# Score tiles of an attention kernel: how five PSUM banks are shared between two passes

## What is computed

```
L1 attention  : softmax(q k^T / sqrt(128)) v, no mask, 16 key heads
L2 attention  : rotary, causal, 16 key heads
L2 ffn, part 1: rotary, causal, 4 key heads (grouped query), then experts
L3 attention  : causal, ALiBi slopes, 4 key heads
L3 ffn        : layer_norm -> w1 (ternary) -> gelu -> layer_norm -> w2 (ternary)
ternary_quant : scale = 1 / clip(mean(|w|), 1e-5); clip(round(w*scale), -1, 1) / scale
```

## Time and profile before

| | |
|---|---|
| median of three runs | 1224.3 us |
| runs | 1224.0 to 1225.42 us |
| span of the profiled execution, first to last instruction | 1215.0 us |
| median of the runs less that span | 9.3 us |
| busy: PE, DVE, ACT, POOL | 1047.8, 841.1, 673.7, 404.6 us |
| mean granted PE clock, share of full | 0.961 |

### The profile page before, as it was taken

One profiled execution on the slowest core, in us unless ns is written; L12 is line 12 of the kernel. 1 busy time (PEld: TensorE's weight loads), 2 busy tenths in 40 slices (PEclk: granted clock), 3 DMA queues, 4 the chain that ended last, 5 costly groups with the idle time before them and its releaser, 6 DMA issues.

```text
span 1215.0 us, 24466 instructions
## 1 busy us (share of the span) xinstructions
PE 1047.8 (86%) x7565; PEld 549.4 (45%) x7640; DVE 841.1 (69%) x2519; ACT 673.7 (55%) x1313; POOL 404.6 (33%) x675
## 2 busy tenths in 40 slices
PE   3468998988889987889999999998989688999886
PEld 1312232322256664445555545554556344555455
DVE  5987878687645557778788787775333766868666
ACT  2217767765754442656666666666556345666553
POOL 5622242222424533442322322334245434222112
PEclk7669999999999999999999999999999889999999
DMA  7235444341112342423412512210233321221001
GB/s 193 68 92 195 131 152 148 125 160 32 33 57 77 92 152 56 130 72 114 131 50 87 184 34 88 77 51 29 79 93 121 93 77 42 88 76 40 2 1 35
DMA packets 100054, 108.03 MB, mean 89 GB/s; under 512 B 10722, under 2 KB 86850, under 8 KB 99688
## 3 DMA queue, kind: packets, MB, share of 16 engines
q1 hardware_dynamic: 83584, 91.91, 24.8%
q0 software_dynamic: 4160, 8.53, 2.5%
q10 hardware_dynamic: 12184, 6.04, 1.7%
HBM read 55.20 MB, written 50.33 MB: 87 GB/s over the span
## 4 chain that ended last, share of the span: by engine, by line
PE 48%; DVE 15%; issue 14%; POOL 7%; ACT 6%; DMA 3%; DVEq 3%; POOLq 2%; SPq 1%; another core or an unknown queue 0%; ACTq 0%
PE bank L2346 10%; PE bank L2331 8%; PE bank L2315 7%; DVE M L1756 5%; POOL SHARED L1164 3%; PE bank L2291 3%; PE bank L2581 3%; PE bank L2333 3%; PE bank L2555 2%; DVE masked_scores L1753 2%; PE bank L2559 2%; ACT PT L1351 2%; DVE N L1539 1%; PE bank L2162 1%; PE bank L2566 1%
## 5 line engine op out<-in xcount | busy, mean ns | idle before, releaser
L1351 ACT ACTIVATE PT<-bank 128x512 f32<-128x512 f32 (+1 forms) x784 | 425.4, 568 | 290.1 <-PE bank L2333 205.4
L2315 PE MATMUL bank<-KS,QS 125*128 125x512 bf16 (+3 forms) x1024 | 310.2, 331 | 38.4 <-DVE M L1756 16.8
L1756 DVE TENSOR_REDUCE M<-bank 128x1 f32<-128x512 f32 (+2 forms) x400 | 260.2, 684 | 88.5 <-PE bank L2315 43.3
L2331 PE MATMUL bank<-QS,KS 128*128 128x256 bf16 (+1 forms) x952 | 278.0, 321 | 14.4 <-ACT PT L1351 11.2
L1753 DVE CUSTOM_DVE_ANT_0 masked_scores<-bank,maskw 128x384 bf16<-128x384 f32 (+1 forms) x384 | 229.4, 621 | 74.8 <-PE bank L2315 65.6
L2346 PE MATMUL bank<-PT,VA 128*32 128x512 f32 (+3 forms) x2048 | 215.5, 493 | 1.4 <-ACT PT L1351 1.0
L2331 PEld LDWEIGHTS bank<-QS,KS 128*128 128x128 bf16 x1024 | 100.1, 99 | 218.1 <-ACT PT L1351 144.5
L2333 PE MATMUL bank<-identb,maskw 128*128 128x128 bf16 x768 | 149.3, 221 | 11.8 <-issue 6.5
L2315 PEld LDWEIGHTS bank<-KS,QS 125*128 125x128 bf16 x1024 | 101.0, 99 | 117.1 <-DVE M L1756 43.8
L1032 POOL CAST MS<-M 128x16 bf16<-128x16 f32 x64 | 13.4, 210 | 277.2 <-DVE M L1756 277.2
L865 POOL TENSOR_TENSOR RSTD<-MS,neg_half 128x4 f32<-128x4 f32 x40 | 42.3, 1056 | 164.1 <-DVE MS L1529 85.9
(11 more groups left out here) (309 smaller groups left out, 1538.3 us busy)
## 6 DMA issues: line engine op xcount, KB each, us to landing
scr_q<-PQ SPq DMA_DIRECT2D x48, 384.0 KB, 3.4
QS<-scr_q SPq DMA_DIRECT2D x64, 288.0 KB
scr_k<-PK SPq DMA_DIRECT2D x24, 384.0 KB, 4.2
KS<-scr_k SPq DMA_DIRECT2D x32, 288.0 KB
slots_x<-XSB SPq DMA_DIRECT2D x32, 256.0 KB, 2.6
XSB<-slots_x SPq DMA_DIRECT2D x92, 64.0 KB
slots_y<-YSB ACTq DMA_DIRECT2D x20, 256.0 KB, 2.4
MW<-in_m_w SPq DMA_DIRECT2D x9, 392.0 KB
```

The lines of the kernel that those rows point to most:

```text
L1351: a.activation(PT[kt % 2][:, js[0]:js[-1] + 1, q0:T], tiles(bank[st_bank(L, g, i)][:, 0:w * len(js)], len(js)), ACT.Exp, scale=c["scale"]) ...
L1756: v.tensor_reduce(M[g % 2][:, t * GH + js[0]:t * GH + js[-1] + 1], tiles(src[:, 0:kl * len(js)], len(js)), AX_X, ALU.max, negate=True).the ...
L2315: r = mm(s, QS[0:ROWS_SHIFT, g * GH + j, t * P:(t + 1) * P], KS[0:ROWS_SHIFT, kv_slot(L, g, j), 0:kl], start=True, stop=not by_pe)
L2331: r = mm(s, KS[:, kv_slot(L, g, j), kt * P:(kt + 1) * P], QS[:, g * GH + j, T - w:T], start=True, stop=not causal)
```

## The change

The max pass gets two banks, 0 and 1, and the transposed pass three, 2, 3 and 5, counted over all items of the kernel. The strict alternation 0, 1, 0, 1 of 11 items begins each causal unit with bank 0 again, which item 10 of the unit before also used. The partition sum of the weights moves from bank 5 to bank 1. Of the three up tiles inside the last unit, the third moves behind the unit, in front of the fourth, and takes bank 2 in place of 5; the fourth takes bank 3 in place of 2. One scratch tile for the masked scores goes.

```diff
-S_ORDER = [[0, 1, 5] * 5 + [1] if n == 16 else ([0, 1, 5] * 4)[:n] for n in NI]
+S_ORDER = [([0, 1] * 8)[:n] for n in NI]
+ST_BANKS = (2, 3, 5)
...
-def st_bank(L, g, i):
-
-    return 2 + (g * NI[L] + i) % 2
+def st_bank(L, b, g, i):
+
+    return ST_BANKS[(item_no(L, b, g) + i) % 3]
+
+
+def item_no(L, b, g):
+
+    return (b * NG + g) * NI[L] + ITEM_BASE[L]
...
-FFN_UP_AT = {(3, 2): 0, (3, 4): 1, (3, 7): 2}
-FFN_BANKS = [(0, 1, 5, 2)] + [(0, 1, 2, 3)] * (NB - 1)
+FFN_UP_AT = {(3, 2): 0, (3, 4): 1}
+FFN_BANKS = [(0, 1, 2, 3)] + [(0, 1, 2, 3)] * (NB - 1)
...
-        masked_scores = {k: sb(f"masked_scores{k}", [P, T], BF16) for k in (0, 1, 5)}
+        masked_scores = {k: sb(f"masked_scores{k}", [P, T], BF16) for k in (0, 1)}
...
-                v.tensor_scalar(qa[:, 0, 2:4], bank[5][:, 0:2], 1.0 / (T * P), 1e-5, ALU.mult, ALU.max).then_inc(qm_used, 1)
+                v.tensor_scalar(qa[:, 0, 2:4], bank[1][:, 0:2], 1.0 / (T * P), 1e-5, ALU.mult, ALU.max).then_inc(qm_used, 1)
...
-                at_least(pe, exp_done, item(L, b, g, i) - 1)
+                at_least(pe, exp_done, item(L, b, g, i) - 2)
...
-                            mm(bank[5][:, 0:2], ones[:, :], qa[:, 0, 0:2], start=True, stop=True).then_inc(qm_ready, 1)
+                            mm(bank[1][:, 0:2], ones[:, :], qa[:, 0, 0:2], start=True, stop=True).then_inc(qm_ready, 1)
...
-            ffn_up_tile(0, NT - 1)
+            for i in range(len(FFN_UP_AT), NT):
+                ffn_up_tile(0, i)
```

More of the change, by code:

```diff
@@ L1351, in unit @@
                         a.activation(PT[kt % 2][:, js[0]:js[-1] + 1, q0:T],
-                                     tiles(bank[st_bank(L, g, i)][:, 0:w * len(js)], len(js)), ACT.Exp,
+                                     tiles(bank[st_bank(L, b, g, i)][:, 0:w * len(js)], len(js)), ACT.Exp,
                                      scale=c["scale"]).then_inc(exp_done, 1)
@@ L2327, in score_t @@
                     pe.wait_ge(shift_landed[g % 2], (half(L, b, g) + 1) * 48)
-                at_least(pe, exp_done, item(L, b, g, i) - 1)
+                at_least(pe, exp_done, item(L, b, g, i) - 2)
                 for n, j in enumerate(js):
-                    s = bank[st_bank(L, g, i)][:, n * w:(n + 1) * w]
+                    s = bank[st_bank(L, b, g, i)][:, n * w:(n + 1) * w]
                     r = mm(s, KS[:, kv_slot(L, g, j), kt * P:(kt + 1) * P], QS[:, g * GH + j, T - w:T], start=True, stop=not causal)
```

## The result

The changed kernel takes 1245.17 us, the median of four runs (1244.67 to 1246.13); the kernel before, on the same chip, took 1224.15 us (1218.17 to 1225.42). The ratio is 1.019, 95% interval [1.0162, 1.0219]: the change made the kernel 1.9% slower. The forecast was 1244.3 us.

What follows compares the result with a forecast made beforehand. TensorE's own stream was taken to bound the causal units, with no engine full in layer 0. The terms 22 + 2 - 3 - 1 = +20 us on 1224.3 gave 1244.3 us, range 1229 to 1260.

Steps and rivals of the forecast that it cites:

- The base: Whole kernel: profiled span 1215.0 us plus the 9.3 us by which the median of the runs lay above it.
- Causal layers, two banks: Layers 1 to 3: scores wait for the reduce two items back, not three; 22 us lost, between 10 and 35.
- Burst A: Unit g=1: VectorE's statistics of the previous block between reduces 6 and 7 delay score 9; loss 1.24 us.
- Burst B: Unit g=2: norm after reduce 2 and second statistics after reduce 5 delay scores 5 and 8; net loss 0.67 us.
- The boundary: Causal unit starts: item 0 shares item 10's bank and waits for the reduce just before; 0.2 us a block.
- the two starting blocks: Causal blocks without a previous block: expert-phase norm, sum and rotation work makes VectorE equally late; priced like the others.
- The third bank: Transposed scores wait for the exponential three items back: 3 us gained in causal layers (0 to 5.8), layer 0 at most 12.
- Layer 0: Two banks cost 1.5 us at the start and 0.5 for the rest: +2 us, between -12 and +18.
- The moved tile: Third up tile leaves the full last unit and fills the gap before the Gelus: -1 us, or 0 if covered.
- Caught up: Rival: TensorE has slack inside units and the 22 us vanish; 1222 us, up to 1232; chance 0.12.
- The exponentials decide: Rival: waits behind ACT matter most, mainly in layer 0, so the kernel gets faster; 1208 us at best; chance 0.07.
- Worse: Rival: nothing in g=2 replaced, layer 0 loses its 14 + 4.5; +52, 1276 us, halfway 1260; chance 0.13.

Runs made afterwards that it cites:

- causal_only: The new banks in layers 1 to 3 and the end alone, layer 0 as before, with the moved tile: 1240.08 us, ratio 1.0137 to the kernel before.
- tile_only: The kernel before with only the third up tile moved behind the last unit: 1223.21 us, ratio 0.9999.
- split_stats: The changed kernel with the previous block's statistics in g=1 cut in three, behind reduces 5, 6 and 7, in layers 1 to 3: 1240.37 us.
- late_stats: The changed kernel with the previous block's statistics in g=1 moved from behind reduce 6 to behind reduce 10, in layers 1 to 3: 1247.36 us.
- start3: The changed kernel with three banks for the first 30 items of layer 0's max pass, bank 5 then handed to the transposed pass: 1240.25 us.
- max3_round: The kernel before with its three maxima banks in unbroken rotation over all items, and the moved tile: 1217.06 us, ratio 0.996.
- max3_split: max3_round with the statistics of unit g=1 cut in three in layers 1 to 3: 1216.77 us, ratio 0.995 to the kernel before.
- max3_stats2: max3_round with the second statistics of unit g=2 moved from behind reduce 5 to behind reduce 8: 1219.02 us, ratio 0.9967 to the kernel before.
- after: The changed kernel itself, 1245.17 us; profiled a second time on another chip it took 1312.56 us, with the kernel before at 1288.12 us there.
- layer0_only: The new banks in layer 0 alone, layers 1 to 3 and the end as before, with the moved tile: 1227.65 us, ratio 1.0039 to the kernel before.
- max2_exp2: The changed kernel without its third bank for the transposed scores, two banks for the maxima: 1253.57 us, ratio 1.0251 to the kernel before.
- no_seam: The changed kernel with the max pass alternating between banks 0 and 1 without a break over all items: 1242.87 us, ratio 1.0169.

## Why the prediction was right, step by step

**The base.** The sum +20 was added to 1215.0 + 9.3. The 9.3 us around the span were mostly a short execution's distance to the median, not time outside the span. The forecast came out right because the medians differ by 21.0; between those two traces it would have been 8 us short. The terms' errors also offset each other: the causal layers, 22 - 3 = 19, were put about 1.5 us too high against causal_only, layer 0 3 us too low. A trace of a kernel with no change in layer 0 (tile_only) is 4.7 us longer than that of before, 1.8 of it up to the end of layer 0's stretch.

**Causal layers, two banks: 22 us, bounds 10 to 35.** Right in mechanism, and in size as far as the traces go. Burst A was 1.24 a block and measured 1.25, its wait stands at the named item behind the named reduce, and split_stats and late_stats both move it. Burst B was 0.67 and measured 0.71: score 5 and 8 wait as said, and score 9's old wait is replaced (0.62 us behind score 8 for the 0.67 assumed). The boundary was 0.2 and measured 0.36, since it costs 0.09 in all four units, not only in the two without a burst. Where the norm stands alone (layer 2's second block) g=2 lost 0.93 us, a little more than the 0.80 that I priced the same. The two traces have +17.6 net; with 3.2 to 4.9 for the third bank that is 21 to 22.5 gross. Two more profiles with the new banks in the causal layers (start3, causal_only) have 3 us more than the changed kernel, none of it in steady units, so the total is known to some 3 us. What the two starting blocks lost, which were priced like the others, can't be read for the same reason.

**The third bank: 3 us in the causal layers, layer 0 bounded by 12.** Measured 3.2 (what repeats) to 4.9, and in layer 0 3.6 to 6.2. The 3 us were about right, though the waits went nearly altogether (11.2 to 1.2) and not by "a little over half". In the steady causal units of layers 1 and 2 it gave nothing, for which the earlier trace rows had the sign: nearly no waits there.

**Layer 0: +2, bounds -12 to +18.** Mis-sized. Measured +5.1 in time. The start was to cost 1.5 and cost 2.7 (against tile_only) to 3.1: I had mixed the clock's two levels as the trace of before had them, and with two banks the whole stretch ran at the lower one. My price for that level, 0.76 us an item and 4.5 in all, was too high in turn: 0.69 us an item was measured. The running units were to cost 0.5 and cost 0.9 (against tile_only) to 2.4, a difference of two larger numbers: without the third bank it would be some 4 to 6 more. Up to 2 us of layer 0's +5.1 may stand in the first experts, which the sum left out.

**The moved tile: -1, bounds -1.08 to 0.** Not confirmed. "After the move everything up to the Gelus is 1.08 us earlier" took TensorE in the last unit as full; from its start to the table load it was busy 10.18 of 12.32 us. The traces give 0.53 us, 0.42 at the end, and the time shows nothing (ratio 0.9999), but can't tell -1 us from none either.

**Rivals.** *Caught up* fell: a steady unit's loss is carried to the end undiminished, unit after unit in the causal layers. Where TensorE waited for a DMA at the start of the next unit, that wait absorbed part of it, as assumed: g=1 lost 0.38 and 0.65 instead of 1.34 in the second and third block of layer 1, where the waits for the shift rows went from 1.41 to 0.45 and from 0.85 us to none. In layer 2's third block g=1 lost only 0.14, but g=2 1.70; the loss came later and was about as large. With *caught up* falls the way in which the prediction used the Trainium skill (Perfetto Trace Analysis, Identifying the Most-Contended Engine): weight loads filled 5.30 of 9.80 us, and there was still no slack to catch up with. The page speaks of how near a kernel is to the roofline; the step from there to slack for a delay was mine. *The exponentials decide* fell: the waits behind ACT vanished as it says, and the kernel was slower. *Worse* fell too. Of the signs named, idle time behind maxima over 50 us (55 to 62), behind exponentials under 6 (1.2), g=1 longer by 1.2 (1.34), g=2 by 0.7 (0.80), g=3 within 0.15 (0.14), a clock that stays (0.98, 1.00, 0.97), and the same length from the end of the last exponential on (54.52 and 54.66 us) came true. The range's lower end, 1229, wasn't what its words gave: half of *caught up* and forecast is 1233.

**Open.** Whether some 2 us of the first experts belong to the change; what makes the DMA wait there vary; what the moved tile is worth; and 0.05 us a block in g=3.

## What to carry over

How many buffers a ring needs is read from the longest stretch in which its consumer does something else, not from the count of waits: the 1.5 us burst of g=1 costs nothing that could be saved with three banks, and 1.25 us with two. Three were not enough for g=2, where a second burst follows three reduces behind the first: there score 9 stood up to 1.02 us even before the change. A ring that doesn't divide the number of items should be counted on over all items. To price a shorter ring, place each producer 0.06 us behind the consumer two back and follow the wait to the next one that it replaces; and look whether the engine that gains the bank idles at all. A burst that is moved instead can move the wait with it, here to POOL and the `shift_t` behind it.

## What the runs showed of the hardware

The clock went with the change. In the stretch from 77 to 87 us every kernel with three banks for these first maxima of layer 0 (before, tile_only, causal_only, max3_round, max3_split, max3_stats2, start3) shows a mean granted clock of 0.59 to 0.78, and every one with two (after in both profiles, layer0_only, max2_exp2, no_seam, late_stats, split_stats) 0.50. What the engine did there differed in the gaps: 18 or 19 matmul records in the two-bank kernels against 21 to 24. The lower clock alone doesn't cost the 2.7 us at the start: max3_round ran its reduces back to back at 0.50.

Two executions of one and the same program, on two chips, differ by no more than 0.01 us in each of 20 units in a row and by 24.0 us in the first experts (152.48 and 176.48 us).
